# Two layers on one core: setup moved into the first stage, a few idle waits filled, work of later stages prepared in earlier ones

## The reference

```
xn = layernorm(x)
# layer 0
s  = xn + softmax(q k^T / scale) v @ w_proj + b_proj       # q, k, v from xn normalised again, scaled and shifted; 16 heads of 8, 1024 x 1024 scores per head
f  = sigmoid(xr @ W_r.T) * (relu(xk @ W_k.T)**2 @ W_v.T)   # xr, xk mix a token with the one before it
# layer 1: landmark attention with 64 landmarks, and 8 experts, 2 per token
L  = softmax(q k_l^T);  K = softmax(q_l k_l^T);  N = softmax(q_l k^T)
P  = K.T / max column sum;  six times  P = P (13 I - KP (15 I - KP (7 I - KP))) / 4
s  = L (P (N v)) @ W_proj
f  = sum over a token's two experts of  weight * (gelu(x W1 + b1) W2 + b2)   # capacity 1075 rows per expert
```

## Time and profile before

| | us |
|---|---|
| median of three runs | 1463.61 (1462.28 to 1465.48) |
| the profiled execution | 1458.4 |
| its span, first to last instruction | 1456.6 |
| PE busy in it | 1285.6 (88%) |
| DVE busy | 1011.4 (69%) |
| ACT busy | 863.6 (59%) |
| POOL busy | 237.3 (16%) |
| mean granted clock of TensorE | 0.929 |

### The profile page before, as it was taken

How to read it: one execution, slowest core, us unless ns; L and a number is a source line. 1 busy time by engine, 2 the same in 40 slices (tenths; PEclk the granted TensorE clock), 3 DMA queues, 4 the chain that set the end, 5 groups by cost and what they waited for, 6 DMA issues and landing times. The chain is left out here.

```text
span 1456.6 us, 26151 instructions
## 1 busy us (share of the span) xinstructions
PE 1285.6 (88%) x10385; PEld 612.0 (42%) x10385; DVE 1011.4 (69%) x1313; ACT 863.6 (59%) x1442; POOL 237.3 (16%) x306
## 2 busy tenths in 40 slices
PE   2876999999999999999999878889899699889990
PEld 2651222222222222222222245545799566568870
DVE  3758898988898988898998455554655488522324
ACT  1541888788787787788888844554223266443331
POOL 4110100000000000000000011000643222124460
PEclk9995999999999999999999977875999599989995
DMA  3575033321334422223200031000010111043316
GB/s 80 177 223 111 14 81 78 72 62 43 73 82 108 107 86 43 63 62 63 61 8 11 5 79 44 16 16 0 3 36 29 32 35 43 12 126 95 94 56 179
DMA packets 75205, 94.97 MB, mean 65 GB/s; under 512 B 13236, under 2 KB 44684, under 8 KB 74052
## 3 DMA queue, kind: packets, MB, share of 16 engines
q1 hardware_dynamic: 69996, 83.19, 22.6%
q0 software_dynamic: 5088, 10.12, 2.2%
HBM read 54.30 MB, written 38.56 MB: 64 GB/s over the span
## 5 line engine op out<-in xcount | busy, mean ns | idle before, releaser
L586 DVE TENSOR_REDUCE b_mx<-psum 128x2 f32<-128x1024 f32 x512 | 601.2, 1218 | 69.4 <-PE psum L667 68.3
L644 ACT ACTIVATE b_exp_ring<-psum 128x512 f32<-128x512 f32 x1024 | 555.5, 599 | 157.2 <-PE psum L703 153.9
L703 PE MATMUL psum<-b_q,b_k 75*128 75x512 bf16 x1024 | 311.3, 386 | 6.7 <-DMA b_q<-b_neg 5.1
L679 PE MATMUL psum<-b_exp_ring,b_v 128*32 128x512 f32 x2048 | 273.5, 606 | 0.9 <-ACT b_exp_ring L644 0.7
L703 PEld LDWEIGHTS psum<-b_q,b_k 75*128 75x128 bf16 x1024 | 79.2, 97 | 321.9 <-ACT b_exp_ring L644 222.8
L665 PE MATMUL psum<-b_k,b_q 64*128 64x512 bf16 x512 | 169.2, 395 | 26.3 <-DVE b_mx L586 13.1
L667 PE MATMUL psum<-b_ko,b_qo 64*128 64x512 bf16 x512 | 169.2, 395 | 0.0
L718 POOL CAST b_neg<-b_neg_rest 16x128 bf16<-16x128 f32 x32 | 9.0, 281 | 660.3 <-DVE b_neg_rest L597 660.3
L665 PEld LDWEIGHTS psum<-b_k,b_q 64*128 64x128 bf16 x512 | 44.4, 93 | 129.3 <-DVE b_mx L586 46.7
L1783 ACT ACTIVATE e_hT<-psum,e_b 128x358 f32<-128x358 f32 (+3 forms) x96 | 53.5, 560 | 74.0 <-PE psum L1803 70.6
L679 PEld LDWEIGHTS psum<-b_exp_ring,b_v 128*32 128x32 f32 x2048 | 41.2, 108 | 108.2 <-issue 106.4
(11 more groups left out here) (275 smaller groups left out, 1503.1 us busy)
## 6 DMA issues: line engine op xcount, KB each, us to landing
b_q<-q_ops SPq DMA_DIRECT2D x48, 192.0 KB
b_k<-k_ops SPq DMA_DIRECT2D x48, 192.0 KB
k_ops<-a_k SPq DMA_DIRECT2D x20, 256.0 KB, 3.2
x_disp<-b_zeros SPq DMA_DIRECT2D x13, 320.0 KB
e_x<-x_disp SPq DMA_DIRECT2D x8, 520.0 KB
v_ops<-a_vs SPq DMA_DIRECT2D x4, 1024.0 KB, 5.5
b_v<-v_ops SPq DMA_DIRECT2D x16, 256.0 KB
av_out<-b_acc SPq DMA_DIRECT2D x128, 32.0 KB, 1.7
```

The lines of the kernel that those rows point to most:

```text
L586: nc.vector.reduce_max(mx[:, d % 2, :, i // 2, i % 2], pair, AX.X).then_inc(sem("b_max_done"), 1)
L644: act.activation(ex[:, n % E_RING, :], g.bank(5 + n % 3), ACT.Exp, scale=ATT_SCALE)\
L679: last = nc.tensor.matmul(AV[32 * i:32 * i + 32, :], v[s][:, at_v:at_v + 32], ex[:, (4 * group + i) % E_RING, :], start=(kb == 0), stop=(k ...
L703: nc.tensor.matmul(g.bank(5 + n % 3), k[s][0:XROWS, h, kb * P:(kb + 1) * P], q[s][0:XROWS, h, half * BANK:(half + 1) * BANK], start=True, ...
```

## The change

It leaves the computation as it is and moves or adds these:

1. `setup` is gone; its work stands in `layer0_inputs`. SP loads the first piece of x, the ten weights, then the other three pieces, each with its own semaphore. `xn(0)` stands between the copies and the scaling of weights on DVE, `stats(1)` behind `zn(0)`.
2. Within a batch PE multiplies wk ahead of wr, and ACT runs ReLU and the second parts ahead of the sigmoid.
3. Five items of row maxima are made at the end of `layer0_inputs` (`FIRST = 5`), the first one between `third` and `pr` of the last batch.
4. In `layer0_outputs` two products of 512 and 256 columns whose result nobody reads (`busy`) stand ahead of the wait for the exponential in `transposed(c, 0)` of couples 1 to 3.
5. The inverse's last product is 64 wide, its DVE factor is left out, z and w go by groups (16 small copies in place of 4), and `klm`, `sums`, `spread` and the first two queries of the second attention are made or loaded there.
6. In the second attention the weights of two experts are loaded at its start and their rows once all tokens are dispatched; the last turn has banks of its own and another order; `yT` has two buffers; a denominator waits for its own step.
7. A one-column Gelu and a one-column Silu stand at the starts of the last two blocks on ACT.

```diff
-            for b in range(B):
-                sp.dma_start(g.X[:, b * TB:(b + 1) * TB, :], xin[:, b * TB:(b + 1) * TB, :])\
+            load_x(0)
+            for i, w in enumerate((g.W_r, g.W_k, g.W_v)):
...
+            sp.dma_start(raw, g.w_qkv[:, :]).then_inc(sem("w_loaded"), 16)
+            for b in range(1, B):
+                load_x(b)
...
             stats(0)
+            dve.wait_ge(sem("w_loaded"), 16 * 10)
+            for c in range(3):
+                nc.vector.tensor_copy(g.wqkv0[:, c, :], raw.rearrange("p (n c) -> p n c", c=3)[:, :, c])
+            link(nc.vector.tensor_scalar(g.cols[:, 4:6], g.cols[:, 2:4], -1.0, 1.0, ALU.mult, ALU.add))
+            xn(0)
+            dve.wait_ge(sem("wT_ready"), 1)
...
+            zn(0)
             stats(1)
-            xn(0)
-            zn(0)
...
                 third(b, 1)
+                if b == B - 1:
+                    first_maximum(0)
                 dve.wait_ge(sem("a_sigr"), b + 1)
                 dve.wait_ge(sem("a_kv"), b + 1)
                 nc.vector.tensor_tensor(pr[:, :], rg[:, :], D3, ALU.mult).then_inc(sem("a_prod"), 1)
...
+                if b == B - 1:
+                    for n in range(1, FIRST):
+                        first_maximum(n)
                 dve.wait_ge(sem("a_sigp"), b + 1)
...
+                else:
+                    pe.wait_ge(sem("b_loaded0"), LOADS0)
+                    pe.wait_ge(sem("a_vs"), B)
+                    first_maxima(0, 1)
                 pe.wait_ge(sem("a_kact"), b + 1)
...
-            for n in range(upto(0, -1)):
+            for n in range(FIRST, upto(0, -1)):
                 item(n)
...
+                def busy(columns):
+                    lo = 0
+                    while lo < columns:
+                        n = min(BANK, columns - lo)
+                        nc.tensor.matmul(D0[:, 0:n], g.wqkv1[:, 0:P], xT[:, 0:n], start=True, stop=True)
+                        lo += n
+
                 def transposed(c, s):
                     k = PAIRS * b + 2 * c + s
-                    pe.wait_ge(sem("c_en"), k + 1)
                     if c:
                         pe.wait_ge(sem("c_enT"), k - 1)
-                    else:
+                        if s == 0:
+                            busy(3 * BANK // 2)
+                    pe.wait_ge(sem("c_en"), k + 1)
+                    if c == 0:
...
+                    if it < B:
+                        (landmarks, ones_of)[stage](it)
-                for n in range(NG):
+                for n in range(NG if it + 1 < ITERS else 0):
...
+                    if it + 1 < ITERS:
+                        squared(n, both_banks(n), x_of, aq_of, "i_mm")
+                    else:
+                        squared(n, both_banks(n)[:, :, LM:P], x_of, q_of, "i_mm")
+            for n in range(NG):
+                pe.wait_ge(sem("i_aq"), at(ITERS - 1, AC, n + 1))
+                squared(n, narrow(2 * n), q_of, lambda p, half: g.NV[half, p, :], "i_z")
+            for n in range(NG):
+                pe.wait_ge(sem("i_z_out"), n + 1)
+                squared(n, narrow(2 * n + 1), lambda p, half: g.KS[half, p, :], lambda p, half: z[half, p, :], "i_w")
...
+            for c in range(2):
+                load_expert(g, sp, c)
+            for k in range(2, TURNS):
+                sp.wait_ge(sem("f_scores"), STEPS * (k - 1))
+                load_queries(g, sp, k)
+            sp.wait_ge(sem("e_set"), 2)
+            sp.wait_ge(sem("dispatched"), 16 * TOPK * NT)
+            for c in range(2):
+                load_rows(g, sp, c)
...
+            pe.wait_ge(sem("f_lx"), 2 * NT)
+            denominators(TURNS - 1, range(STEPS - 1))
             transposed(NT - 1)
-            for k in range(TURNS - 2, TURNS):
-                for stage, turn in stages:
-                    if STEPS * (k + 1) + turn >= NT:
-                        stage(k)
+            spread_wide(TURNS - 2)
+            denominators(TURNS - 1, range(STEPS - 1, STEPS))
+            numerators(TURNS - 1)
+            outputs(TURNS - 2)
+            spread_wide(TURNS - 1)
+            outputs(TURNS - 1)
...
+            act.activation(spare[:, :], g.eps_pow[:, 0:1], ACT.Gelu).then_inc(sem("e_spare"), 1)
```

More of the change, by code:

```diff
@@ L467, in _ @@
                 rows_times(nc, D0, znT, g.wqkv0[:, 2, :]).then_inc(sem("a_v"), 1)
-                for t in range(TB):
-                    dst = D1[:, t * P:(t + 1) * P]
-                    nc.tensor.matmul(dst, now[:, t * P:(t + 1) * P], g.wr2[0][:, :], start=True, stop=False)
-                    last = nc.tensor.matmul(dst, before[:, t * P:(t + 1) * P], g.wr2[1][:, :], start=False, stop=True)
-                last.then_inc(sem("a_r"), 1)
                 pe.wait_ge(sem("a_res"), 2 * b + 1)
@@ L478, in _ @@
                 last.then_inc(sem("a_kk"), 1)
+                for t in range(TB):
+                    dst = D1[:, t * P:(t + 1) * P]
+                    nc.tensor.matmul(dst, now[:, t * P:(t + 1) * P], g.wr2[0][:, :], start=True, stop=False)
+                    last = nc.tensor.matmul(dst, before[:, t * P:(t + 1) * P], g.wr2[1][:, :], start=False, stop=True)
+                last.then_inc(sem("a_r"), 1)
                 if b + 1 < B:
                     transposed_x(b + 1)
+                else:
+                    pe.wait_ge(sem("b_loaded0"), LOADS0)
+                    pe.wait_ge(sem("a_vs"), B)
+                    first_maxima(0, 1)
                 pe.wait_ge(sem("a_kact"), b + 1)
@@ L1402, in _ @@
                     pe.wait_ge(sem("i_x"), at(it, XS, 2 * NG + n + 1))
-                    squared(n, both_banks(n), x_of, aq_of, "i_mm")
-            pe.wait_ge(sem("i_aq"), AC * ITERS)
-            for p in range(NPAIR):
-                for half in halves:
-                    last = nc.tensor.matmul(narrow(0)[half, p, :], AQ[half, p, LM:P], g.NV[half, p, :],
-                                            start=True, stop=True)
-            last.then_inc(sem("i_z"), 1)
-            pe.wait_ge(sem("i_z_out"), 1)
@@ L1412, in _ @@
-            for p in range(NPAIR):
-                for half in halves:
-                    last = nc.tensor.matmul(narrow(1)[half, p, :], g.KS[half, p, :], z[half, p, :], start=True, stop=True)
-            last.then_inc(sem("i_w"), 1)
-STEPS = 4
-TURNS = NT // STEPS
-SPAN = STEPS * P
+                    if it + 1 < ITERS:
+                        squared(n, both_banks(n), x_of, aq_of, "i_mm")
+                    else:
+                        squared(n, both_banks(n)[:, :, LM:P], x_of, q_of, "i_mm")
@@ L1888, in _ @@
         def _(act):
+            act.activation(spare[:, :], g.eps_pow[:, 0:1], ACT.Silu).then_inc(sem("g_spare"), 1)
             for i in range(PARTS):
```

333 lines of the change are left out of this document (167 added, 166 removed).

## The result

The changed kernel takes 1402.95 us (median; 1400.87 to 1405.03), the kernel before, measured beside it, 1462.94: a ratio of 0.959 (0.957 to 0.961), 60.0 us less. Its profiled execution took 1400.87 (span 1399.1, mean granted clock 0.954 for 0.929). From span to span the difference is 57.5 us, and it divides without a rest into nine stretches whose ends both traces have.

| stretch | before | after | difference | predicted |
|---|---|---|---|---|
| start to first q product | 31.07 | 17.88 | -13.2 | -12.3 |
| to q product of batch 3 | 57.26 | 53.98 | -3.3 | -4.2 + 2.5 |
| to the first scores | 48.39 | 47.95 | -0.4 | -1.9 |
| first attention, to the first transposes of x | 703.47 | 706.14 | +2.7 | 0 |
| layer 0's outputs, to the inverse's first product | 182.15 | 161.52 | -20.6 | -18 |

What follows compares the result with a forecast made beforehand. The prediction saw the time in dips of TensorE's granted clock. Terms summing to 52.8 us took the profiled 1458.4 to 1405.6, or 1410.8 on the median's scale; the forecast's own range was 1402 to 1420, widened to 1398 to 1429.

Steps and rivals of the forecast that it cites:

- Start: Layer 0's inputs: reordered loads bring the first q product 12.3 us earlier, less 2.5 for slow first products: -9.8 us.
- Order within a batch: Layer 0's inputs: kv's wait of 1.50 us goes, 1.4 stays won in each of three batches: -4.2 us.
- Five maxima: First attention's entry: block ends 1.4 us later, but scores start 24.1 after the border, gaining 3.3: -1.9 us.
- Throw-away columns: Layer 0's outputs: columns fill the waits, so the clock holds in batches 0 to 2: -18 us.
- End of the inverse: Inverse's last product, z and w: a 64-wide product and no wait before z end it earlier: -5.5 us.
- Entry of the second attention: Second attention's first scores: masks, ones and queries are ready, so most of the 5.85 us wait goes: -4.0 us.
- its end: Second attention's last turn: with own banks, denominators and spread no longer queue behind outputs: -3.5 us.
- Experts' entry: Experts' first transposes: loads hidden in the block before, table load moved beside the transposes: -5.9 us.
- Rival 3: First attention: entered after a wait, its clock fails to rise; slower than before, for instance 1495 us; chance 0.02.
- Rival 4: Outputs and inverse: the clock holds in batch 3 too and z and w run fast: 1401 us; chance 0.10.

Runs made afterwards that it cites:

- e12: The changed kernel itself, run again unaltered beside the third group of follow-up kernels: 1399.38 us, ratio 0.958.
- e11: Changed kernel plus maxima's store between quad loads and added columns at first attention's entry, batch 3's first couple and second attention's first steps: 1398.92 us, ratio 0.957.
- e4: The kernel before with the throw-away columns in layer 0's outputs added as its only change: 1445.68 us, ratio 0.990.
- e1: The changed kernel with the throw-away columns in layer 0's outputs taken out: 1419.61 us, ratio 0.971.
- e3: The changed kernel with the loads of quads 1 and 2 issued in the block before, behind batch 2's stores: ratio 0.961.
- e9: The changed kernel with the first maxima's store issued between the loads of quads 1 and 2, not behind both: ratio 0.959.

## Why the prediction was right, and where it was not

The time fell as forecast and for the forecast's main reason; the gain was 5 (between the spans) to 7 us (between the medians) larger than the 52.8 of the sum. Step by step:

- **Start (-9.8; came out at -11.2).** First q product at 17.88, not 18.8; batch 0 took 19.34 and the next 17.32, so the slow first products cost 2.0 and not 2.5. Mechanism and sizes held. (One reading was off: from 18.64 to 21.32 are 2.7 us, not 2.5. That these products ran at half clock is read from durations, as said above.)
- **Order within a batch (-4.2; -5.3).** kv's wait is gone and batches take 17.32 for 19.09: 1.77 each for the 1.4 I left after ACT's delay.
- **Five maxima (-1.9; -0.4).** The term that was mis-sized. Its first half held: the border, where the loads start, came 1.2 us later for the 1.4 forecast (22.1 for 21.0 from batch 3's q product). That is the four items on DVE (4.6 us, 87.90 to 92.43) less what the new order and DVE's wait gave back; with one early item it is 18.8. The second half did not: scores came 25.8 after the border where I had 24.1 (and 27.4 before), a gain of 1.6 and not 3.3. The store was issued 16.4 after the border, as forecast, but the loads ahead of it ended 24.4 after it and not 23.4, and the scores started 1.4 behind their end and not 0.7. Since the loads start at the border, all that delays the border delays the scores: one early item, with the border 3.5 earlier, gives scores at 116.70 without any wait, so the four moved items cost 3.5 and gave 0.4. That comparison the forecast did not make. The Trainium skill, "DMA: Bandwidth & Descriptors", Queues, rings and completion order, was the right page, and the landings of 8.4 and 1.7 agree with its ring order.
- **Throw-away columns (-18; -20.6).** As told: clock 1.00 over batches 0 to 2 from 850 on (batch 0 still begins at 0.50, in 826 to 830, as the forecast did not say, and in e12 it fell once more at that batch's end), couples of 5.74, half clock only behind batch 3's wait of 2.55, back within its second couple; 19.9 with the columns taken out (181.4 less 161.5) and 20.3 with them put in alone (182.2 less 161.8). The reason, "a gap of 1.6 brings it down", is only mostly true: one batch of three passed two such gaps before it fell. The size was low because I charged batch 3 with 12 us of half clock and it had about 7 (0.7, 4 and 2.1 us in the stretches of clock 0.91, 0.50 and 0.74); 5 us at 31% are 1.6 of the 2.6 missing, and the stage's own spread is wider than the rest.
- **End of the inverse (-5.5; -8.6).** The last product and the wait saved 4.5, as worked out. z took 3.85 for the 5.2 assumed and w 5.45 for 7.0. Both were the good end of a spread: without an edit there, other kernels had up to 2.2 more.
- **Entry of the second attention (-4.0; -4.1)** and **its end (-3.5; -4.3)** held. A term was missing between them: the steps up to the last dispatch took 111.88 for 109.76, since the clock, fallen in w, came back 25 us after the first scores and not 13. (In e11, with columns there and the clock back after 14, it was 110.37.) The waits that an entry loses do not all come back as time when its work then runs at 1.2 GHz.
- **Experts' entry (-5.9; -7.4).** Loads hidden, table load beside the transposes. What the term left out is the clock: before, it had fallen in the last turn's output products (0.58 in 1272 to 1274), ahead of the wait of 5.65, and the transposes behind it took 2.24; now it is 1.00 from 1220 to 1230 and they take 1.26. Which part of the last turn's new order keeps it up was not tried.
- **Rival 3** had a grain of truth. The first attention did lose 2.7 us: 1.2 in its first two steps, and more at places such as 540.19, where a wait of 1.49 for a maxima's store was followed by a clock of 0.60 in 540 to 544. Before, a wait of 1.54 at 555.94 passed at 1.00. Across the fourteen traces here, whose loops are the same, this stretch took 702.4 to 709.3. The kernel of e4, which is that of before but for the columns, took 707.3. So it is a spread, and no effect of the change on it is shown; my sum gave it no width. Rival 4 (1401) came nearest in time, and nearer than the forecast's 1410.8, but only by half of its mechanism: z and w ran faster than assumed, while batch 3's clock did fall. The measured 1402.95 lies near the lower end of the forecast's own range of 1402 to 1420; the outputs and the inverse were at the good ends of their spreads in the profiled execution.

## What to carry to other kernels

Where an engine's clock falls at short waits, look for the waits that recur, and put work nobody reads into the part of them that is idle: here it needed no other change and, where it stuck out of the wait, cost no more than that. In the couples where it filled the wait it held the clock in every trace here; at bringing a fallen clock back it helped in two places and failed in a third. Before moving work ahead of a barrier, ask which transfers start behind the barrier and whether the thing you speed up queues behind them; the order of issue gave here what four moved items did not. And when terms of 2 to 3 us are to be judged, compare stages in two traces, since a stretch nobody edited moved by as much.

## What the runs showed of the hardware

- The granted clock is partly chance: in one execution (e1) the first gap of 1.6 us brought it down in two batches and the third gap in another, and in the first attention a single wait of 1.49 did so (0.60 in 540 to 544 of the changed kernel) where one of 1.54 did not (1.00 behind 555.94 of the kernel before).
- A fallen clock does not rise merely because TensorE has no idle time: 17 us without a gap in the profile at the first attention's entry (107 to 124 in e11), 128-column products between the items up to 118, stayed at 1.2 GHz. The Trainium skill, "TensorE: Matmul & The Clock Gate", What's actually happening, has activity release the throttle; here that fits the columns in batch 3's second couple (clock back at about 964) and in the second attention's steps (14 us for 21 to 25), and not this stretch. What sets the two apart is open.
- Issuing one of the quads' loads or of the maxima's stores on SP took 0.3 to 0.6 us as a rule. In e3, with 26 loads issued just before and DMA busy all the time (share 0.87 to 1.02 from 74 to 94), single issues took up to 4, and SP's own lateness then moved the block's border.
- On the chip of the second group the same 256 products of the inverse took 8.8 us (e9) in place of 7.6, with idle of 0.4 put down to issue, and the kernel before took 1471.59: only ratios and stages can be compared across groups.
